# A two-layer message-passing kernel on one core: tiles processed 14 quads behind their visits, and the normalisation of message rows moved from VectorE to ScalarE

## The chip, the cores and the metric

The kernel runs on 1 core of one Trainium2 chip. The metric is the device time of that core in microseconds (us), as the median of the runs of one kernel. Times inside the kernel come from one profiled execution. The engines are named as in the profile: PE (TensorE matmul), PEld (its weight load), DVE (VectorE), ACT (ScalarE), POOL (GpSimd), SP (the engine that issues most DMAs); SPq, POOLq are their queues.

## The reference

A graph has 6,250 nodes with rows of 256 floats and 106,250 edges, sorted by destination, each with one weight. The first layer computes, for each edge, a message from the rows of both ends and the weight, sums messages by `src`, and updates the nodes:

```python
msg = silu(concat(h[src], h[dst], d2) @ mW1 + mb1)
msg = layer_norm(msg, ln_g, ln_b)
msg = silu(msg @ mW2 + mb2)
agg = segment_sum(msg, src, num_segments=6250)
y = silu(concat(h, agg) @ uW1 + ub1) @ uW2 + ub2
x = layernorm(x + (h + y))
# second layer: mean over the edges of x[src], by dst
agg = segment_sum(x[src], dst) / max(counts, 1)
x = layernorm(x + relu(agg @ W.T + b))
```

## The kernel before, in words

**Tiles, visits, quads.** The edges are cut into 831 tiles of 128, one edge to a partition; four tiles make a quad, and there are 208 quads of tiles (`TILE_QUADS`). The nodes are cut into 50 blocks of 125 (`BLOCKS`). A tile of sorted edges meets one or more blocks; each meeting is a "visit", of which there are 880, in 220 quads (`QUADS`). Tile t is complete once visit t + 49 is done (`BEHIND`).

**Preparation (0 to 222 us).** SP loads edges and weights, writes zeros into four sum tables in DRAM, and loads x. DVE and PE work out visits, blocks and ring slots (`vslot`, `vslot0`). Then `pq_step` runs over the 50 blocks: PE transposes x and multiplies it by both halves of mW1; the src half P goes to the table `p_tab` in DRAM, the dst half Q stays in SBUF as three bf16 parts in `big`. Last, SP issues `s_wrow`, a DMA that copies three partitions of the split weight row to three partitions of `big`, 50 times over (L407). POOL starts its gathers after `s_wrow`, after all stores of P, and after `s_q3`.

**First stage (222 to 2982 us), `step_0` and `message_loop`.** Each engine runs the same software pipeline in its own program order.

- POOL (`gather_0`, `add`): for each quad of tiles four indirect DMAs (L531) fetch P rows by src into a ring `ring0` of 60 slots; four indirect DMAs (L542) later add the finished rows `tot` into the four sum tables, by row numbers `sidx`. Gather g waits for the adds-in of quad g-4 (`pre`) and, once the ring is full, for the silu of the quad that held its slots.
- SP (`place_rows`): for each quad of visits it loads a row of local node numbers, copied to 125 partitions (`lrow`, L415), and three weight rows (L417).
- DVE: `one_hot` (L1234) makes the one-hot matrix; `add_in` (L1250) adds PE's result of a visit to its ring slot, four adds to a quad; `norm` takes `bn_stats` (L1259) of four silu'd rows, an inverse root by three Newton steps, and four `tensor_scalar` (L1282) that subtract the mean and scale; `count_before` (L1292) and `sum_rows` find duplicate source nodes and make `sidx`.
- PE: `norm_columns` (L701, transposes of the normalised rows), `sum_same` (L691), `expand` (L715: 12 matmuls that expand Q rows to the visit's edges), `keys` (L681), `main` (L727, L728: the product with mW2).
- ACT: two `silu` halves (L900), between them two evictions of transposes (L921), `total` (L936), `compare` (L910, L913), `message` (L928, the second silu).

At step q DVE adds in visit quad q + LAG and then normalises tile quad q; LAG is 13, so a tile quad is processed right after the add-in that completes it: `silu` of quad q waits for the `add_in` that DVE does at the same step. `expand` waits for all four adds of the visit quad before it, and signals once for all four.

**The rest (2982 to 4574 us).** The node update, the second layer's gathers and sums over the same visits (L570, L817, L1446), its projection, and the stores. The weight W of the second layer is loaded and transposed at the start (`wl`, `wt`, L597, L864).

Of the kernel before, what the change touches and what calls it, by code (L numbers as in the profile page):

```python
# [15 lines left out]
D = 256  # L16
# [29 lines left out]
RING0 = 60  # L46
RING0_QUADS = RING0 // QT
LAG = -(-BEHIND // QT)
assert RING - BEHIND < 4 * QT and RING0_QUADS == LAG + 2
# [3 lines left out]
def gnn(nc, x, src, dst, edge_w, mW1, mb1, ln_g, ln_b, mW2, mb2, uW1, ub1, uW2, ub2, W, b, out):  # L53
# [13 lines left out]
    with ExitStack() as ctx:  # L67
# [14 lines left out]
        wt = sb("wt", [P, H, D])  # L82
        b2r = sb("b2r", [P, D], bf16)
        blb = sb("blb", [P, D])
# [4 lines left out]
        RING0_W = RING0 * D  # L89
# [3 lines left out]
        ring0 = arena[:, BIG_W:BIG_W + RING0_W].rearrange("p (s d) -> p s d", s=RING0)  # L93
# [10 lines left out]
        vblk, vslot, vslot0, tslot = (vtab[32 * i:32 * i + 1, :] for i in range(4))  # L104
# [54 lines left out]
        wl = cut([H, D])  # L159
# [23 lines left out]
        region(LATE, 2048)  # L183
# [3 lines left out]
        ub2b = cut([D])  # L187

# [8 lines left out]
        nwt = sb("nwt", [P, 2, 4, QT])  # L197

# [33 lines left out]
        def by_place(rows_, group):  # L232
# [29 lines left out]
                 "keys", "silu", "bst", "mom", "newt", "norm", "ztr", "zev", "mm", "msg", "ded", "tot", "added"],  # L262
# [85 lines left out]
        def _(sp):  # L348
# [10 lines left out]
            for dest, arr in ((w1, mW1[0:2 * D, :]), (w2, mW2), (wl, W)):  # L359
                sp.dma_start(dest[:, :, :], arr.rearrange("(k p) d -> p k d", p=P)).then_inc(s_weights, 16)  # L360
            for dest, row in ((w1cf[:, 0, :], mW1[2 * D:2 * D + 1, :]), (b1b[:, :], mb1), (b2f[:, 0, :], mb2),
                              (blb[:, :], b)):
# [16 lines left out]
            def pq_step(q, k):  # L379
# [13 lines left out]
                if isinstance(q, int) and q == 0:  # L393
                    store_places()

            def store_places():
# [10 lines left out]
            sp.dma_start(big[NB:P, :, :, :].rearrange("p j k d -> p j (k d)"),  # L407
                         w1cp[0:PARTS, :, :].rearrange("p k d -> p (k d)").unsqueeze(1)
                         .to_broadcast([PARTS, BLOCKS, PARTS * D])).then_inc(s_wrow, 16)
            sp.wait_ge(s_vtab, 16 * 2 * (1 + PARTS))  # L410

            def place_rows(v, par):
                if later(v, 2):
                    sp.wait_ge(e[0]["qexp"], v - 1)
# [176 lines left out]
        def _(pe):  # L591
# [115 lines left out]
            def expand(q, par, blocks_):  # L707
# [3 lines left out]
                if later(q, 1):  # L711
                    pe.wait_ge(s["pre"], QT * q)
# [784 lines left out]
```

## Time and profile before

| | |
|---|---|
| median of 3 runs | 4588.72 us (4584.3 to 4591.06) |
| profiled execution, its own time | 4576.25 us |
| its span, first to last instruction | 4574.4 us |
| PE busy | 3282.8 us, 72% |
| POOL busy | 3025.7 us, 66% |
| DVE busy | 2739.4 us, 60% |
| ACT busy | 1443.1 us, 32% |
| mean granted TensorE clock | 0.858 of full speed |

Busy time is averaged over stages that have different limits; a stage has to be read by itself. The idle time in brackets ahead of an instruction names what ended it; "issue" means that the engine waited for nothing that the profile shows.

### The profile page before, as it was taken

How to read it: one execution, taken by the hardware profiler on the slowest of the kernel's cores; microseconds unless marked ns; L12 is line 12 of the kernel's file. 1: busy time of each engine (PE TensorE's matmuls, PEld its weight loads, DVE VectorE, ACT ScalarE, POOL GpSimd, SP SyncE). 2: the span in 40 equal slices, each digit the busy share in tenths (PEclk: the TensorE clock that was granted, in tenths of full speed). 3: DMA queues.
4: the chain of work that ended last, by engine and by line, in shares of the span. 5: the costliest groups of instructions: out<-in, count | busy, mean ns of one | idle time of the engine just before them, and what ended most of it. 6: DMA issues, size and time to landing. Idle time of an engine off the chain costs nothing. (4 is left out here: it accounts for less than half of the span.)

```text
span 4574.4 us, 77539 instructions
## 1 busy us (share of the span) xinstructions
PE 3282.8 (72%) x16047; PEld 2382.8 (52%) x16048; DVE 2739.4 (60%) x11915; ACT 1443.1 (32%) x2712; POOL 3025.7 (66%) x2631
## 2 busy tenths in 40 slices
PE   5737777777777777777777778686666666666675
PEld 2326666665656666666666666575333333343344
DVE  5437766666666666666666667567444444444455
ACT  0304444444444444444444445432000000000004
POOL 0057888888888888888888886521666666666634
PEclk8959888898989998888889889998777787777788
DMA  8335555555555555555555555754333333333313
GB/s 285 101 87 90 92 92 94 92 92 93 92 92 92 93 92 92 93 93 92 93 93 92 92 93 76 116 156 141 91 90 90 89 90 89 89 90 89 90 53 114
DMA packets 335844, 453.23 MB, mean 99 GB/s; under 512 B 53568, under 2 KB 282524, under 8 KB 335772
## 3 DMA queue, kind: packets, MB, share of 16 engines
q0 software_dynamic: 199680, 327.32, 38.4%
q1 hardware_dynamic: 136092, 125.14, 9.2%
q8 instruction: 22, 0.36, 0.0%
q14 instruction: 50, 0.41, 0.0%
HBM read 296.41 MB, written 155.62 MB: 99 GB/s over the span
## 5 line engine op out<-in xcount | busy, mean ns | idle before, releaser
L542 POOL DMA_INDIRECT sum<-arena,sidx x832 | 1327.9, 1596 | 320.3 <-issue 252.5
L531 POOL DMA_INDIRECT arena<-p_tab,esrc x832 | 819.9, 985 | 507.9 <-issue 249.9
L570 POOL DMA_INDIRECT arena<-x_tab,esrc x832 | 795.5, 956 | 473.7 <-issue 195.2
L817 PE MATMUL ps<-arena 128*125 x1760 | 696.9, 485 | 474.1 <-DVE arena L1446 249.6
L691 PE MATMUL ps<-arena 128*128 128x256 f32 x1664 | 560.4, 496 | 454.2 <-ACT arena L928 454.2
L727 PE MATMUL ps<-w,arena 128*128 128x256 f32 x3328 | 833.9, 383 | 17.5 <-ACT arena L936 17.4
L817 PEld LDWEIGHTS ps<-arena 128*125 128x125 f32 x1760 | 386.0, 237 | 771.0 <-issue 707.5
L1446 DVE TENSOR_TENSOR arena<-ps,arena 125x257 f32 x880 | 374.8, 426 | 617.1 <-remote 234.6
L691 PEld LDWEIGHTS ps<-arena 128*128 128x128 f32 x1664 | 389.2, 245 | 560.7 <-issue 495.7
L727 PEld LDWEIGHTS ps<-w,arena 128*128 128x128 f32 x3328 | 567.3, 190 | 136.9 <-issue 20.1
L910 ACT ACTIVATE arena<-ps,key 128x128 f32<-128x128 f32 x832 | 237.9, 369 | 1118.0 <-remote 1114.4
L1259 DVE BATCH_NORM_STATS2 bst<-arena 128x6 f32<-128x256 f32 x832 | 313.0, 418 | 389.5 <-ACT arena L900 384.9
L1250 DVE TENSOR_TENSOR arena<-ps,arena 128x256 f32 x880 | 372.9, 424 | 233.5 <-DVE arena L1250 84.4
L715 PE MATMUL ps<-arena 128*128 x2640 | 419.6, 322 | 83.0 <-DVE arena L1250 64.5
L991 ACT ACTIVATE arena<-ps 128x250 f32<-128x250 f32 x50 | 18.7, 375 | 1309.0 <-DVE cnt L1462 1309.0
L715 PEld LDWEIGHTS ps<-arena 128*128 128x128 bf16 x2640 | 309.0, 117 | 208.6 <-issue 117.0
L820 PE MATMUL ps<-identh 128*128 128x512 bf16 x880 | 399.3, 454 | 0.0
L1282 DVE TENSOR_SCALAR arena<-arena,mom,nwt 128x256 f32<-128x256 f32 x832 | 317.8, 442 | 99.9 <-DVE nwt L332 89.8
L701 PE MATMUL ps<-ident,arena 128*128 128x128 f32 x1664 | 228.4, 281 | 133.3 <-DVE arena L1282 108.9
L921 ACT ACTIVATE arena<-ps,gb 128x512 f32<-128x512 f32 x416 | 319.8, 769 | 7.8 <-PE ps L701 7.7
L701 PEld LDWEIGHTS ps<-ident,arena 128*128 128x128 f32 x1664 | 187.8, 143 | 186.0 <-DVE arena L1282 116.7
L900 ACT ACTIVATE arena<-arena 128x512 f32 x416 | 258.2, 621 | 35.1 <-DVE arena L1250 27.7
(177 smaller groups left out, 3927.8 us busy)
## 6 DMA issues: line engine op xcount, KB each, us to landing
arena<-loc_tab SPq DMA_DIRECT2D x220, 125.0 KB
sum<-arena SPq DMA_DIRECT2D x4, 6400.0 KB
arena<-sum SPq DMA_DIRECT2D x200, 128.0 KB, 2.1
arena<-p_tab,esrc POOLq DMA_INDIRECT x832
sum<-arena,sidx POOLq DMA_INDIRECT x832
arena<-x_tab,esrc POOLq DMA_INDIRECT x832
arena<-x_tab SPq DMA_DIRECT2D x50, 128.0 KB, 2.0
arena<-in_x_dram SPq DMA_DIRECT2D x50, 112.0 KB
```

The source lines that it names most:

```text
L531: pool.indirect_dma_start(out=ring0[:, tile % RING0, :], out_offset=None, in_=p_tab[:, :], in_offset=bass.IndirectOffsetOnAxis(ap=esrc[:, ...
L542: pool.indirect_dma_start(out=sums[u][:, :], in_=tot[:, par, u, :], in_offset=None, out_offset=bass.IndirectOffsetOnAxis(ap=sidx[:, par, u ...
L570: pool.indirect_dma_start(out=ring[:, tile % RING, 0:D], out_offset=None, in_=x1_tab[:, :], in_offset=bass.IndirectOffsetOnAxis(ap=esrc[:, ...
L691: last = nc.tensor.matmul(ps[:, PM + u // 2, u % 2 * D:(u % 2 + 1) * D], same[:, par, u, :], msg[:, par, u, 0:D], start=True, stop=True)
L701: last = nc.tensor.transpose(ps[:, PZ + h, u * P:(u + 1) * P], act[:, par, u, h * P:(h + 1) * P], ident[:, :])
L715: last = nc.tensor.matmul(ps[:, PP + u // 2, u % 2 * D:(u % 2 + 1) * D], hott[:, par, u, :], big[:, bass.ds(blocks_[u], 1), i, :].rearrang ...
L727: nc.tensor.matmul(to, zt[:, par, h, u * P:(u + 1) * P], w2[:, h, :], start=h == 0, stop=False)
L817: nc.tensor.matmul(ps[0:NB, u, 0:CW], same1[:, par, u, :], ring[:, bass.ds(at[u], 1), :].rearrange("p a c -> p (a c)"), start=True, stop=T ...
L820: nc.tensor.matmul(ps[:, PK, :], identh[:, :], identh[:, :].unsqueeze(1).to_broadcast([P, QT, P]), start=True, stop=True)
L921: nc.scalar.activation(zt[:, par, h, :], ps[:, PZ + h, :], ACT.Identity, bias=gb[:, h, 1:2], scale=gb[:, h, 0:1]).then_inc(s["zev"], 1)
L1250: nc.vector.tensor_tensor(row, ps[:, PP + u // 2, u % 2 * D:(u % 2 + 1) * D], row, ALU.add)\
L1446: nc.vector.tensor_tensor(row, ps[0:NB, u, 0:CW], row, ALU.add).then_inc(s["acc"], 1)
```

## The change

The lag between visits and tiles grows from 13 to 14 quads (`LAG`), and the ring from 60 to 64 slots, so that both layers share one table of slots. `silu` of a quad now waits for the add-in of DVE's previous step. `expand` waits and signals by pairs of visits (one PSUM bank each), and `add_in` takes them by pairs. DVE no longer applies the normalisation: it computes one small `shift` = -mean times scale, and ACT applies scale and shift with four activations, placed after `compare` and ahead of `message`. W, its transposes, its eviction and its bias move from the start to behind the first stage. The copy of the weight row (`s_wrow`) is issued in `store_places`, at block 0 of `pq_step`, rather than after block 49; the first two `place_rows` are issued at block 46.

```diff
-RING0 = 60
-RING0_QUADS = RING0 // QT
-LAG = -(-BEHIND // QT)
+LAG = -(-BEHIND // QT) + 1
@@ sync
-            for dest, arr in ((w1, mW1[0:2 * D, :]), (w2, mW2), (wl, W)):
+            for dest, arr in ((w1, mW1[0:2 * D, :]), (w2, mW2)):
...
+                if isinstance(q, int) and q == BLOCKS - 4:
+                    sp.wait_ge(s_vtab, 16 * 2 * (1 + PARTS))
+                    for v in range(2):
+                        place_rows(v, v)
@@ store_places
+                sp.wait_ge(s_wpart, 5)
+                sp.dma_start(big[NB:P, :, :, :].rearrange("p j k d -> p j (k d)"),
+                             w1cp[0:PARTS, :, :].rearrange("p k d -> p (k d)").unsqueeze(1)
+                             .to_broadcast([PARTS, BLOCKS, PARTS * D])).then_inc(s_wrow, 16)
@@ after the last block of pq_step
-            sp.wait_ge(s_wpart, 5)
-            sp.dma_start(big[NB:P, :, :, :].rearrange("p j k d -> p j (k d)"),
...
...
-            for dest, arr in ((u1, uW1), (u2, uW2)):
+            for dest, arr in ((u1, uW1), (u2, uW2), (wl, W)):
@@ gather_0
-                if g >= RING0_QUADS:
-                    pool.wait_ge(e[0]["silu"], 2 * (g - RING0_QUADS + 1))
+                if g >= RING_QUADS:
+                    pool.wait_ge(e[0]["silu"], 2 * (g - RING_QUADS + 1))
@@ expand (PE)
-                if later(q, 1):
-                    pe.wait_ge(s["pre"], QT * q)
                 for u in range(QT):
+                    if u % 2 == 0 and later(q, 1):
+                        pe.wait_ge(s["pre"], QT * q - 2 + u)
...
-                last.then_inc(s["qexp"], 1)
+                    if u % 2:
+                        last.then_inc(s["qexp"], 1)
@@ after the message loop (PE)
+            pe.wait_ge(s_late, 16 * 6)
+            pe.wait_ge(s["same"], TILE_QUADS)
+            for kd in range(H):
+                for kh in range(H):
+                    last = nc.tensor.transpose(ps[:, PK, (kd * H + kh) * P:(kd * H + kh + 1) * P],
+                                               wl[:, kh, kd * P:(kd + 1) * P], ident[:, :])
+            last.then_inc(s_wtr, 1)
+            pe.wait_ge(s_wt, 1)
@@ silu (ACT)
-                    ac.wait_ge(s["pre"], QT * (q + LAG + 1) if not isinstance(q, int) else QT * min(q + LAG + 1, QUADS))
+                    ac.wait_ge(s["pre"], QT * (q + LAG) if not isinstance(q, int) else QT * min(q + LAG, QUADS))
@@ ACT
+            def norm(q, par):
+                ac.wait_ge(s["shift"], q + 1)
+                for u in range(QT):
+                    last = nc.scalar.activation(act[:, par, u, :], act[:, par, u, :], ACT.Identity,
+                                                bias=shift[:, par, u:u + 1], scale=nwt[:, par, 3, u:u + 1])
+                last.then_inc(s["norm"], 1)
...
                 if live(q, TILE_QUADS):
                     compare(q, par)
+                if live(q, TILE_QUADS):
+                    norm(q, par)
                 if live(q - 1, TILE_QUADS):
                     message(q - 1, 1 - par)
@@ add_in (DVE)
-                dve.wait_ge(s["qexp"], v + 1)
                 for u in range(QT):
+                    if u % 2 == 0:
+                        dve.wait_ge(s["qexp"], 2 * v + 1 + u // 2)
@@ norm (DVE)
-                for u in range(QT):
-                    last = nc.vector.tensor_scalar(act[:, par, u, :], act[:, par, u, :], m[:, 4, u:u + 1],
-                                                   nwt[:, par, 3, u:u + 1], ALU.subtract, ALU.mult)
-                last.then_inc(s["norm"], 1)
+                nc.vector.scalar_tensor_tensor(out=shift[:, par, :], in0=m[:, 4], scalar=-1.0, in1=nwt[:, par, 3],
+                                               op0=ALU.mult, op1=ALU.mult).then_inc(s["shift"], 1)
```

## Rows read from the trace of the kernel before

**Rows 1.** The page: busy us, share of the span, and instructions of each engine.

```profile
PE 3282.8 (72%) x16047; PEld 2382.8 (52%) x16048; DVE 2739.4 (60%) x11915; ACT 1443.1 (32%) x2712; POOL 3025.7 (66%) x2631
```

**Rows 2.** Windows: us; busy of PE, PEld, DVE, ACT, POOL; PEclk, DMA share, GB/s.

```profile
222.50:351.90 129.40, 53.23 (x273) 35.26 (x274) 48.55 (x169) 13.15 (x24) 64.76 (x68) 0.59 0.31 86
351.90:2803.20 2451.30, 1889.77 (x10761) 1500.65 (x10762) 1686.50 (x8655) 1181.90 (x2117) 1981.16 (x1532) 0.90 0.56 92
2803.20:2982.00 178.80, 127.87 (x761) 102.57 (x758) 113.26 (x599) 86.31 (x150) 101.90 (x65) 0.93 0.62 96
```

**Rows 3.** Groups of POOL, 351.9 to 2803.2 us: busy, mean ns, idle before, releaser.

```profile
L542 POOL DMA_INDIRECT sum<-arena,sidx x768 | 1226.0, 1596 | 240.4 <-issue 233.9 <-ACT arena L936 6.6
L531 POOL DMA_INDIRECT arena<-p_tab,esrc x764 | 755.1, 988 | 232.8 <-issue 232.8
```

**Rows 4.** Timeline around 1400 us: start, us, instruction, idle before it.

```profile
1400.29 1.53 DVE L1282 TENSOR_SCALAR arena<-arena,mom,nwt 128x256 f32<-128x256 f32 x4 [0.87 <-DVE nwt L332]
1401.58 1.69 POOL L542 DMA_INDIRECT sum<-arena,sidx  x1 [0.30 <-issue]
...
1414.45 1.58 POOL L542 DMA_INDIRECT sum<-arena,sidx  x1 [0.30 <-issue]
```

**Rows 5.** Timeline: one `total` on ACT in the steady part.

```profile
1447.62 1.02 ACT L936 ACTIVATE arena<-ps 128x1024 f32<-128x1024 f32 x1 [0.79 <-DMA sum<-arena,sidx]
```

**Rows 6.** Timeline: from the last block of `pq_step` to the first gather.

```profile
209.81 0.93 SPq L407 DMA_DIRECT2D arena<-arena  x1
210.05 0.42 ACT L882 ACTIVATE arena<-arena 125x256 bf16<-125x256 f32 x1 [0.27 <-DVE arena L1207]
210.50 0.42 DVE L1213 TENSOR_TENSOR arena<-arena 125x256 bf16<-125x256 f32 x1 [0.24 <-ACT arena L882]
...
217.85 2.00 SPq L417 DMA_DIRECT2D arena<-wgt_tab  x1
222.51 1.18 POOL L531 DMA_INDIRECT arena<-p_tab,esrc  x1 [216.55 <-DMA arena<-arena]
```

**Rows 7.** DMA queue of SP, 211 to 222.2 us: packets, MB, share of 16 engines.

```profile
q1 hardware_dynamic: 364, 0.44, 18.3%
```

**Rows 8.** Timeline: the first blocks of `pq_step`.

```profile
96.08 0.58 SPq L403 DMA_DIRECT2D wgt_tab<-arena  x1
98.20 0.78 SPq L391 DMA_DIRECT2D p_tab<-arena  x2
101.61 0.42 DVE L1204 TENSOR_TENSOR arena<-ps,arena 125x256 f32<-125x256 f32 x1 [0.21 <-PE ps L667]
```

**Rows 9.** Waits of POOL, 222 to 352 us: us in total, times, longest.

```profile
POOL arena L531 <- ACT arena L900: 23.6, 2, 18.3
POOL arena L531 <- DVE arena L1250: 17.9, 9, 6.7
```

**Rows 10.** Timeline: first adds of visit quads 2, 12, 13; `expand` of quad 13.

```profile
256.77 0.42 DVE L1250 TENSOR_TENSOR arena<-ps,arena 128x256 f32 x1 [16.59 <-remote]
...
320.17 0.42 DVE L1250 TENSOR_TENSOR arena<-ps,arena 128x256 f32 x1 [1.90 <-PE ps L715]
...
322.58 2.74 PE L715 MATMUL ps<-arena 128*128 x12 [2.62 <-DVE arena L1250]
...
325.53 0.42 DVE L1250 TENSOR_TENSOR arena<-ps,arena 128x256 f32 x1 [2.18 <-PE ps L715]
```

**Rows 11.** Timeline after the last gather: POOL's first scatter of three quads; ACT, PE.

```profile
2835.47 1.68 POOL L542 DMA_INDIRECT sum<-arena,sidx  x1 [3.20 <-DVE sidx L1311]
2835.89 1.03 ACT L928 ACTIVATE arena<-ps 128x1024 f32<-128x1024 f32 x1 [2.53 <-PE ps L728]
2842.20 1.10 PE L727 MATMUL ps<-w,arena 128*128 128x256 f32 x4 [1.21 <-ACT arena L936]
2909.19 1.68 POOL L542 DMA_INDIRECT sum<-arena,sidx  x1 [2.99 <-DVE sidx L1311]
2974.77 1.55 POOL L542 DMA_INDIRECT sum<-arena,sidx  x1 [3.05 <-DMA sum<-arena,sidx]
```

More of the change, by code:

```diff
@@ L103, in gnn @@
         vtab = sb("vtab", [P, VISITS], i32)
-        vblk, vslot, vslot0, tslot = (vtab[32 * i:32 * i + 1, :] for i in range(4))
+        vblk, vslot, tslot = (vtab[32 * i:32 * i + 1, :] for i in range(3))
         esrc = sb("esrc", [P, CHUNKS * P], i32)
@@ L187, in gnn @@
         ub2b = cut([D])
+        wl = cut([H, D])
+        wt = cut([H, D])
+        blb = cut([D])
         scr = sb("scr", [P, QT, P])
@@ L197, in gnn @@
         nwt = sb("nwt", [P, 2, 4, QT])
+        shift = sb("shift", [P, 2, QT])
         tnum_i = sb("tnum_i", [P, CHUNKS], i32)
@@ L261, in gnn @@
         EDGE = [["gat0", "gat1", "gat2", "gat3", "loc0", "loc1", "wgt0", "wgt1", "hott", "keyt", "apart", "same", "dup", "dif", "sidx", "qexp", "pre",
-                 "keys", "silu", "bst", "mom", "newt", "norm", "ztr", "zev", "mm", "msg", "ded", "tot", "added"],
+                 "keys", "silu", "bst", "mom", "newt", "shift", "norm", "ztr", "zev", "mm", "msg", "ded", "tot", "added"],
                 ["hot", "agg", "acc"]]
@@ L394, in pq_step, with place_rows @@
                     store_places()
+                if isinstance(q, int) and q == BLOCKS - 4:
+                    sp.wait_ge(s_vtab, 16 * 2 * (1 + PARTS))
+                    for v in range(2):
+                        place_rows(v, v)
+            def place_rows(v, par):
+                if later(v, 2):
+                    sp.wait_ge(e[0]["qexp"], 2 * (v - 1))
+                sp.dma_start(lrow[0:NB, par, :], loc_tab[:, bass.ds(v * (QT * P), QT * P)].to_broadcast([NB, QT * P]))\
+                    .then_inc(e[0][f"loc{par}"], 16)
+                sp.dma_start(hott[NB:P, par, :, :].rearrange("p u n -> p (u n)"),
+                             wgt_tab[:, bass.ds(v * (QT * P), QT * P)]).then_inc(e[0][f"wgt{par}"], 16)
             def store_places():
@@ L592, in _ @@
             pe.wait_ge(s_const, 10)
-            pe.wait_ge(s_weights, 16 * 11)
-            for kd in range(H):
-                for kh in range(H):
-                    last = nc.tensor.transpose(ps[:, PK, (kd * H + kh) * P:(kd * H + kh + 1) * P],
-                                               wl[:, kh, kd * P:(kd + 1) * P], ident[:, :])
-            last.then_inc(s_wtr, 1)
-            pe.wait_ge(s_wt, 1)
+            pe.wait_ge(s_weights, 16 * 9)
             def tile_before(tile, prev):
@@ L862, in _ @@
         def _(ac):
-            ac.wait_ge(s_wtr, 1)
-            nc.scalar.activation(flat(wt[:, :, :]), ps[:, PK, :], ACT.Copy).then_inc(s_wt, 1)
             def pq_step(q, par):
@@ L952, in step_0 @@
                     compare(q, par)
+                if live(q, TILE_QUADS):
+                    norm(q, par)
                 if live(q - 1, TILE_QUADS):
                     message(q - 1, 1 - par)
-            ac.wait_ge(s_weights, 16 * 11)
+            ac.wait_ge(s_weights, 16 * 9)
             ac.wait_ge(s_constc, 8)
             message_loop(ac, step_0)
+            ac.wait_ge(s_wtr, 1)
+            nc.scalar.activation(flat(wt[:, :, :]), ps[:, PK, :], ACT.Copy).then_inc(s_wt, 1)
             t = k[0]
```

71 lines of the change are left out of this document (28 added, 43 removed).

## The prediction

> **What bounds the kernel now.** I read the page first: over the whole span PE is the busiest engine, at 72%, and POOL comes behind it at 66% [rows 1]. That average hides the answer, so I cut the span into windows by stage [rows 2] and then asked for POOL's groups in the long middle of the first stage [rows 3]. The two groups are 1226.0 + 755.1 us of work and 240.4 + 232.8 us of gaps, together 2454 us in a window of 2451.3: POOL does nothing but issue indirect DMAs. All but 6.6 us of its gaps are "issue", 466.7 us over 1532 instructions, 0.30 us each. It never waits there for a gather slot, for `tot` or for `sidx`. From the first scatter (351.9) to that of quad 192 (2803.2) are 192 iterations of 2451.3 / 192 = 12.77 us: 4 scatters of 1.596, 4 gathers of 0.988 and 8 gaps. The rest follows POOL: ACT's `total` is let go by the landing of a scatter [rows 5], which means that the chain of DVE, ACT and PE is ahead by as much as its buffers allow.
>
> Two short parts are not bound so. At the head, from the first gather to the first scatter (129.4 us, [rows 2]), POOL does 17 quads of gathers at 64.76 / 68 = 0.95 us and a gap of 0.30 each, so 5.0 us a quad and 85 in all; 44 us are idle, and [rows 9] name who is late: `silu` of quads 0 and 1 (23.6) and the adds-in (17.9), each with the usual gap in it; the rest is the first `total`. After the last gather the scatters wait 3 us a quad [rows 11]: from quad 195 (2835.47) to quad 202 (2909.19) are seven periods of 10.53 us. There the chain is the bound. The second layer is not touched.
>
> So the question for each part of the change is when POOL starts, what its iterations cost, and how long the chain takes at either end.
>
> **1. The start of the gathers.** Before, `pq_step` ends at 210.92 on DVE, but POOL starts at 222.51, let go by the copy L407, issued at 209.81 [rows 6]. From issue to release are 12.7 us. While it runs, SP's queue uses 18.3% of 16 DMA engines [rows 7], close to 3/16 = 18.8%: three engines, one per partition copied. The loads that SP issues behind it are held up as well (L417 takes 2.00 us to issue, [rows 6]). The Trainium skill ("DMA: Bandwidth & Descriptors", section on why a DMA increments its semaphore by 16) says that the number of engines is the largest up to 16 that divides the slowest dimensions, and that each engine takes its descriptors in ring order; the share in the trace agrees.
>
> After, the same copy is issued in `store_places`, behind the last `wgt_tab` store (96.08 to 96.66, [rows 8]), ahead of the load of block 4 and the store of block 0, both of which also use these three engines. So it is paid there: issued at 96.7, it ends, by its 12.7 us, at 109.4. The store of block 0, issued at 98.20 now, frees the buffer that DVE needs for block 2 at 101.61 [rows 8]. That add moves to about 109.8: 8.2 us later. Nothing in `pq_step` catches up, since 48 blocks from there to 210.50 take 2.27 us each [rows 6, 8]. Removing the load of W and its bias (384 KB) from the queue ahead of four zeroed tables of 6.6 MB each, which is 1.5% of what must pass in the 85 us or so before the x rows, gives 1.2 back. The gathers then wait for the last store of P, about 1 us after DVE: 210.9 + 8.2 - 1.2 + 1 = 218.9 instead of 222.5. **-3.5 us.** Bounds: -11.5 if the copy is hidden in `pq_step`, 0 if it delays by all 12. PE's four transposes and ACT's eviction at the start lie beside the zero fill, and the slot arithmetic that DVE drops too: 0. At their new place they lie beside POOL's last scatters: 0; uncovered, 2 us.
>
> **2. The head.** Visits go in lockstep now: four adds, then 12 matmuls that wait 2.62 us for them and take 2.74 [rows 10], at a granted clock of 0.59 [rows 2], near the lower level of 1.2 GHz: 5.36 us a quad (320.17 to 325.53). By pairs the two overlap: 1.0 us of adds, 1.4 of matmuls and 0.6 of signals for a pair, 3.0 us for a quad. POOL's 5.01 becomes the pace. The stalls stay: quad 2 is added in only at 256.77 after 16.59 us of "remote" [rows 10], and others of 2 to 5 us every third quad; why, no row tells. Adds of quad 13 end some 2.2 us after their start at 325.53, at 327.7, 105 us after the first gather. With the stalls kept and catching up at 3.0, I get 81.5 us if only the first counts (34 + 8 quads x 5.01 + landing and adds) and 101 if each stall comes at its old time. I take 90, nearer the middle. From there to the first scatter are 24.2 us, two passes of the chain, which term 4 shortens by about a tenth: 22. Head: 112 instead of 129.4, **-17.4**, bounds -4 and -28. One more gather quad lies inside it, in POOL's idle time.
>
> **3. POOL's iteration.** DVE's four L1282 disappear. [Rows 4] show that a scatter which starts while they run takes 1.69 us, and one in the next iteration, which starts as they start, 1.58: 0.11 for a hit. One hit in two iterations to one in each gives 0.055 to 0.11; I take 0.077, so 12.69 us. 190 iterations: **-14.6**; bounds 0 (the hit moves to another DVE instruction) and -30. Here the Trainium skill speaks up ("SBUF — State Buffer", section "SBUF: two separate sides"): a DVE instruction in a two-port mode keeps GpSimd off the shared port for the whole instruction, so it can't write descriptors. By that rule 1.53 us of L1282 in each iteration could be up to 290 us in the stage; the row says 0.11 per hit.
>
> ACT's share grows: a 256-wide activation takes 0.42 us alone [rows 6]; four in a row 1.2 to 1.7, I take 1.4. ACT is busy 1181.9 / 192 = 6.2 us of 12.77 [rows 2]; 7.6 after. `message` of the quad before is queued behind it, and `sum_same` on PE waits for that. Covered: POOL's pace leaves the chain at least 12.77 - 10.53 = 2.2 us an iteration. The lag itself buys nothing here, since nobody waits for the chain.
>
> **4. The tail.** Its loop now: DVE's adds, `silu`, statistics, Newton, L1282 (1.4 to 1.5 us for four, [rows 4]), and on ACT and PE `message`, `sum_same`, `total`, then `main`, which waits 1.21 us for `total` [rows 11]. After, `silu` no longer waits for adds (about 1.7 us), and DVE sheds 1.3. From one `main` to the next: message 1.03, two silus and two evictions 2.9, total 1.0 with its signals, and 4.14 of matmuls make 9.25; but statistics 0.75, Newton to `shift` 4.2 and ACT's 1.4 behind the second silu end at 9.55. I take 9.55 (bounds 9.2 and 10.3). Before, from the scatter of quad 190 to that of 207 (2974.77) are 2 x 12.77 + 171.6 = 197.1 us, with 14.8 beyond the regular period while x rows are loaded. After, one quad more is without gathers: 10 + 16 x 9.55 + 14.8 = 177.6. **-19.5**, bounds -8 and -24.
>
> **Sum.** -3.5 - 17.4 - 14.6 - 19.5 = -55. Against the profiled execution: its own time 4576.25 becomes 4521, span 4519. The median of the runs is 12.5 us above that execution; I take the same difference for the change: 4588.7 - 55 = **4534**.
>
> **Rivals.**
> A. Only the ends give a little: POOL's iteration stays at 12.77 and the stalls of the head come at their old times: -3.5 - 4 - 0 - 12 = -20, **4569**. For it: the stalls had no cause in view, and other DVE instructions can hit. 0.20.
> B. POOL was slowed by DVE in more than the visible hits. Its floor by the means of the windows with least beside them is 4 x 1.57 (101.90 / 65 in the tail) + 4 x 0.95 (64.76 / 68 in the head) + 8 x 0.30 = 12.48 [rows 2], so -55 in place of -14.6: **4493**. 0.08. This is how far the skill's rule on the shared port could come in; full exclusion would have to show in [rows 4], and doesn't.
> C. Slower: DVE, free of its waits, settles where L1292, L1234 and the small operations fall on POOL's starts. Each hit costs 0.11 or more; the ends give 40 us, so it decides from 0.21 us an iteration, two hits more than now. At three new hits of 0.12 and the old one lost, +0.28 an iteration is +54 us, less the 40 of the ends: 14 slower than before, **4603**. Against it: those instructions exist today at all phases, and the mean is only 0.29 above that floor. 0.04.
> D. Nothing measurable: the early copy holds `pq_step` by more than 12 us, the head's stalls grow by what the pairs save, and the tail stays bound by `main`: -8, **4581**. 0.10.
> That the lag does nothing by itself in the steady part is in every case.
>
> **Numbers.** Forecast 0.58, A 0.20, B 0.08, C 0.04, D 0.10. About 0.2% (9 us) is what a measurement of this kernel can tell. Faster: forecast, A, B, which is 0.86, less 0.01 for A's edge: 0.85; same 0.11; slower 0.04. The forecast's own range, from the bounds in part: 4507 to 4560. To leave out no more than 2 in 10 it must hold A: 4500 to 4574.
>
> **What would show it.** The page after: POOL's first gather near 219; the copy's engines busy near 98 to 110 and DVE waiting there for a store of P; DVE's visits at 5.0 us or less a quad in the head; first scatter near 331; POOL's steady groups still with "issue" gaps only, means 1.57 to 1.59 and 0.98; tail periods near 9.6 us; ACT near 1730 us busy, DVE near 2400. Wrong would make it: POOL waiting for `tot` or `sidx` in the steady part, a period off 12.69 by more than 0.1, or a head as long as now.

## The result, and the profile after

The changed kernel takes 4685.88 us (median of 4 runs, 4681.7 to 4699.55). The kernel before takes 4589.89 beside it (4 runs, 4584.3 to 4591.94). That is a ratio of 1.0222, 95% interval 1.0209 to 1.0234. It is 2.2% slower. The forecast was 4534 and faster.

The page of the profiled execution has a span of 4685.7 us and these busy times, to be held against [rows 1]:

```profile
PE 3327.0 (71%) x16047; PEld 2460.8 (53%) x16048; DVE 2462.8 (53%) x11287; ACT 1859.4 (40%) x3544; POOL 3008.0 (64%) x2631
```

Work moved from DVE to ACT as foretold, and POOL is even 18 us less busy. So nothing became longer on POOL; it waited more. The windows by stage say where: first gather to first scatter, then to the last gather, then to the copy of the x rows (us; busy of PE, PEld, DVE, ACT, POOL; PEclk, DMA share, GB/s).

```profile
220.55:346.93 126.38, 57.41 (x282) 36.48 (x283) 47.30 (x166) 17.04 (x31) 68.50 (x73) 0.59 0.34 93
346.93:2886.17 2539.24, 1878.83 (x10643) 1537.50 (x10641) 1416.97 (x7993) 1548.76 (x2850) 1946.51 (x1519) 0.86 0.54 88
2886.17:3091.42 205.25, 153.40 (x879) 123.88 (x876) 111.59 (x636) 132.34 (x241) 113.19 (x73) 0.90 0.60 93
```

The middle holds 190 iterations: 2539.24 / 190 = 13.36 us each, where [rows 2] give 12.77. POOL's groups in it (busy, mean ns, idle before, releaser), beside [rows 3]:

```profile
L544 POOL DMA_INDIRECT sum<-arena,sidx x760 | 1202.5, 1582 | 366.9 <-issue 223.4 <-ACT arena L945 143.5
L533 POOL DMA_INDIRECT arena<-p_tab,esrc x759 | 744.0, 980 | 231.3 <-issue 231.0 <-DMA sum<-arena,sidx 0.3
```

Each scatter got shorter, 1582 ns for 1596 (why is another matter, see step 3 below), and 143.5 us of waits for ACT's `total` (L945) appeared where there were 6.6. POOL no longer sets the pace in every iteration; in 37 of about 120 between 1000 and 2600 us it waits for the chain of ACT, PE and DVE. The list of waits, 1000 to 2600 us (total us, times, longest), shows its links:

```profile
ACT arena L912 <- remote: 440.2, 77, 7.1
PE ps L697 <- ACT arena L921: 409.7, 87, 6.7
...
POOL sum L544 <- ACT arena L945: 86.6, 37, 3.4
```

L912 is `compare`, L921 the normalisation, L697 PE's transposes of the normalised rows. "Remote" means that the trace shows no instruction ending just before the wait ended. The timeline of two steps tells what that wait is:

```profile
1418.87 1.14 ACT L912 ACTIVATE arena<-ps,key 128x128 f32<-128x128 f32 x4 [6.43 <-remote]
1420.05 0.72 ACT L915 ACTIVATE arena<-arena,onesf 128x512 f32<-128x512 f32 x1
1420.68 2.06 ACT L921 ACTIVATE arena<-arena,shift,nwt 128x256 f32<-128x256 f32 x4
1422.64 1.00 ACT L937 ACTIVATE arena<-ps 128x1024 f32<-128x1024 f32 x1
1422.79 1.97 PE L697 MATMUL ps<-ident,arena 128*128 128x128 f32 x8 [5.80 <-ACT arena L921]
...
1424.55 2.90 PE L687 MATMUL ps<-arena 128*128 128x256 f32 x8
1427.29 1.47 PE L711 MATMUL ps<-arena 128*128 x12
1428.60 0.61 PE L677 MATMUL ps<-identh,keyh 128*128 128x128 bf16 x8
...
1432.45 1.14 ACT L912 ACTIVATE arena<-ps,key 128x128 f32<-128x128 f32 x4 [3.85 <-remote]
```

PE's keys matmuls (L677) end at 1429.21, and `compare`, which waits for them, begins at 1432.45, 3.24 us later; the one before began 5.84 us late (its matmuls are at 1412.42, 0.61 long). Behind `compare` in ACT's queue stands the normalisation, 2.06 us, and PE waits for that: a ring, keys, `compare`, normalisation, L697, `sum_same`, `expand`, keys. From `compare` at 1418.87 to keys at 1428.60 is 9.73 us, so one turn is that, 0.61 of keys, and the lateness. The lateness is not the same in every step: between 1000 and 2600 us it is under 1.3 us in 36 of 120.

From all rows of `compare` and of the keys matmuls in that window, the mean turn comes apart into two parts. In the kernel before, 7.85 us from the start of `compare` to the end of the next keys, and 4.94 of lateness, make 12.78, which is POOL's own iteration. In the changed kernel it is 9.91 and 3.45, which make 13.36. So the ring took in 2.06 us, the length of the normalisation, and the lateness gave 1.49 of them back.

By stage, up to the last scatter (before, then after): first gather 222.51, 220.55; head 129.4, 126.4; last scatter 2980.36, 3089.82. So 109 of the 111 us that the span grew lie ahead of the last scatter: 114 between the first scatter and the last, less the 5 gained ahead of the first. That the ring turns too slowly because the normalisation stands behind a late `compare` is called Theory A below. Theory B is that the 14 quads behind or the two signals a quad cost it.

### The profile page after: what moved, and what is told of

Same layout as the page of the kernel before. It is cut to its first block and busy times, and to the rows that moved or that the text cites. A ratio compares the mean times of both kernels' runs of the same rounds, so it can differ in the third digit from the quotient of the medians.

```text
span 4685.7 us, 78432 instructions
## 1 busy us (share of the span) xinstructions
PE 3327.0 (71%) x16047; PEld 2460.8 (53%) x16048; DVE 2462.8 (53%) x11287; ACT 1859.4 (40%) x3544; POOL 3008.0 (64%) x2631
## 5 line engine op out<-in xcount | busy, mean ns | idle before, releaser
L821 PE MATMUL ps<-arena 128*125 x1760 | 716.8, 497 | 447.4 <-DVE arena L1457 214.8
L697 PE MATMUL ps<-ident,arena 128*128 128x128 f32 x1664 | 330.1, 363 | 690.4 <-ACT arena L921 682.3
L821 PEld LDWEIGHTS ps<-arena 128*125 128x125 f32 x1760 | 403.1, 245 | 749.0 <-issue 680.9
L697 PEld LDWEIGHTS ps<-ident,arena 128*128 128x128 f32 x1664 | 261.0, 187 | 770.4 <-ACT arena L921 581.9
L912 ACT ACTIVATE arena<-ps,key 128x128 f32<-128x128 f32 x832 | 237.7, 368 | 789.1 <-remote 689.3
L687 PEld LDWEIGHTS ps<-arena 128*128 128x128 f32 x1664 | 417.9, 264 | 100.2 <-issue 24.4
L921 ACT ACTIVATE arena<-arena,shift,nwt 128x256 f32<-128x256 f32 x832 | 428.3, 585 | 30.6 <-DVE shift L1294 29.6
L824 PE MATMUL ps<-identh 128*128 128x512 bf16 x880 | 412.9, 469 | 0.0
L711 PE MATMUL ps<-arena 128*128 x2640 | 351.1, 286 | 68.4 <-DVE arena L1263 45.2
L711 PEld LDWEIGHTS ps<-arena 128*128 128x128 bf16 x2640 | 269.4, 102 | 147.0 <-issue 82.7
L945 ACT ACTIVATE arena<-ps 128x1024 f32<-128x1024 f32 x208 | 212.9, 1024 | 213.3 <-PE ps L687 128.9
```

Source lines behind the costliest of these rows:

```text
L687: last = nc.tensor.matmul(ps[:, PM + u // 2, u % 2 * D:(u % 2 + 1) * D], same[:, par, u, :], msg[:, par, u, 0:D], start=True, stop=True)
L697: last = nc.tensor.transpose(ps[:, PZ + h, u * P:(u + 1) * P], act[:, par, u, h * P:(h + 1) * P], ident[:, :])
L711: last = nc.tensor.matmul(ps[:, PP + u // 2, u % 2 * D:(u % 2 + 1) * D], hott[:, par, u, :], big[:, bass.ds(blocks_[u], 1), i, :].rearrang ...
L821: nc.tensor.matmul(ps[0:NB, u, 0:CW], same1[:, par, u, :], ring[:, bass.ds(at[u], 1), :].rearrange("p a c -> p (a c)"), start=True, stop=T ...
L824: nc.tensor.matmul(ps[:, PK, :], identh[:, :], identh[:, :].unsqueeze(1).to_broadcast([P, QT, P]), start=True, stop=True)
L921: last = nc.scalar.activation(act[:, par, u, :], act[:, par, u, :], ACT.Identity, bias=shift[:, par, u:u + 1], scale=nwt[:, par, 3, u:u + 1])
```

## The experiments

The runs came on different chips, and that turned out to be part of the finding. I call the chip of the result A; B to F are five chips of the later runs, all different. Which chip A is was not noted. B, C, D and F give the kernel before other times than A does, but E gives nearly the same and may be the same chip. Each ratio is against the kernel before on the same chip. "POOL" is its iteration: the window 1000 to 2600 us has so many POOL instructions, 8 to an iteration, so 12800 over their number. "Late" is from the end of the keys matmuls to `compare`, 1000 to 1400 us, mean; it is left out where it was not taken, or (norm first) where ACT's own order makes it. In e6 ACT's own order makes the 1.1 too. The runs of e9 to e12 are two each.

| run | chip | us | before there | ratio (95%) | POOL | late |
|---|---|---|---|---|---|---|
| kernel before | A | 4589.89 | | 1 | 12.76 | 5.0 |
| changed kernel | A | 4685.88 | 4589.89 | 1.0222 (1.0209 to 1.0234) | 13.38 | 3.5 |
| e1 norm on DVE | B | 4360.52 | 4373.23 | 0.9968 (0.9955 to 0.998) | 12.70 | 0.1 |
| e2 before, ACT norm | B | 4367.43 | 4373.23 | 0.9986 (0.9977 to 0.9996) | 12.71 | |
| e3 norm first | B | 4351.51 | 4373.23 | 0.9949 (0.9932 to 0.9965) | 12.64 | |
| e4 one signal | B | 4355.25 | 4373.23 | 0.9954 (0.9937 to 0.997) | 12.65 | |
| e5 changed kernel | C | 4352.32 | 4373.67 | 0.9949 (0.9932 to 0.9966) | 12.65 | 0.1 |
| e6 kernel before | C | 4372.89 | 4373.67 | one run | 12.76 | 1.1 |
| e7 changed, 2 loads | C | 4382.08 | 4373.67 | 1.0019 (1.0009 to 1.003) | 12.66 | 2.9 |
| e8 before, 2 loads | C | 4362.81 | 4373.67 | 0.9973 (0.9963 to 0.9983) | 12.71 | 3.1 |
| e9 changed, 4 loads | D | 5464.07 | 4555.83 | 1.1994 (1.1959 to 1.2029) | 17.02 | 6.1 |
| e10 norm first, 4 loads | D | 4907.1 | 4555.83 | 1.0771 (1.0688 to 1.0855) | 14.24 | 5.4 |
| e11 DVE norm, 4 loads | D | 4972.25 | 4555.83 | 1.0914 (1.0832 to 1.0996) | 14.68 | 6.3 |
| e12 before, 4 loads | D | 5020.21 | 4555.83 | 1.102 (1.0976 to 1.1063) | 14.78 | 6.1 |
| e13 changed kernel | E | 4697.18 | 4583.2 | 1.0257 (1.0239 to 1.0274) | 13.36 | 3.6 |
| e14 kernel before | E | 4586.41 | 4583.2 | one run | 12.77 | 4.9 |
| e15 norm first | E | 4583.8 | 4583.2 | 1.0004 (0.9995 to 1.0014) | 12.83 | |
| e16 norm on DVE | E | 4578.64 | 4583.2 | 0.9988 (0.9978 to 0.9998) | 12.79 | 4.9 |
| e17 keys last | F | 4755.99 | 4372.28 | 1.0877 (1.0859 to 1.0895) | 14.50 | 0.1 |
| e18 one signal | F | 4351.75 | 4372.28 | 0.9954 (0.9937 to 0.997) | 12.64 | 0.1 |

**e1, e2, e3, e4: the parts.** The edits, each by itself (e2 on the kernel before, the others on the changed one):

```diff
@@ e1: L1294 back to DVE's four instructions, and no norm on ACT
-                nc.vector.scalar_tensor_tensor(out=shift[:, par, :], in0=m[:, 4], scalar=-1.0, in1=nwt[:, par, 3],
-                                               op0=ALU.mult, op1=ALU.mult).then_inc(s["shift"], 1)
+                for u in range(QT):
+                    last = nc.vector.tensor_scalar(act[:, par, u, :], act[:, par, u, :], m[:, 4, u:u + 1],
+                                                   nwt[:, par, 3, u:u + 1], ALU.subtract, ALU.mult)
+                last.then_inc(s["norm"], 1)
@@ e2: the reverse of e1, in the kernel before, norm(q, par) behind compare(q, par)
@@ e3: step_0 of ACT
                 if live(q, TILE_QUADS):
-                    compare(q, par)
-                if live(q, TILE_QUADS):
                     norm(q, par)
+                if live(q, TILE_QUADS):
+                    compare(q, par)
@@ e4: expand and add_in, one wait and one signal a quad
-                    if u % 2 == 0 and later(q, 1):
-                        pe.wait_ge(s["pre"], QT * q - 2 + u)
+                    if u == 0 and later(q, 1):
+                        pe.wait_ge(s["pre"], QT * q)
...
-                    if u % 2:
-                        last.then_inc(s["qexp"], 1)
+                    if u == QT - 1:
+                        last.then_inc(s["qexp"], 2)
...
-                    if u % 2 == 0:
-                        dve.wait_ge(s["qexp"], 2 * v + 1 + u // 2)
+                    if u == 0:
+                        dve.wait_ge(s["qexp"], 2 * v + 2)
```

> The changed kernel, with the normalisation given back to VectorE (four tensor_scalar a quad, no shift, no norm on ScalarE); lag 14, 64 slots, pairs and the moved DMAs stay. Theory A (ScalarE's normalisation is queued behind compare, which starts late, and makes the chain of DVE, ACT and PE longer than POOL's iteration): POOL has only its 0.30 us gaps again, an iteration is about 12.75 us against 13.37, and the time is 4575 to 4592. Theory B (the new lag and the signals by pairs disturb the chain): it stays at about 4680.

> The kernel before, with only the normalisation moved to ScalarE, in the place that the change gives it (after compare, ahead of message); lag 13, 60 slots. Theory A: as slow as the changed kernel or slower, 4680 to 4800, since silu still waits for the adds-in of its own step. Theory B: about 4590, the same as before.

> The changed kernel, with ScalarE's norm placed ahead of compare instead of behind it; nothing else. Theory A: the late start of compare no longer holds up the normalisation, so much of the loss comes back: iteration 12.8 to 13.1, time 4590 to 4640. If it is only ScalarE's 2.06 us of work and not the place, or theory B: 4670 to 4700.

> The changed kernel, with expand waiting and signalling once for all four visits again, and the adds-in waiting once. Theory A: within 10 us of the changed kernel's 4686, perhaps a little slower at the head. Theory B: back towards 4590.

Measured: all four took 0.1 to 0.5% less than the kernel before, and in all four POOL's gaps are its usual 0.3 us. On chip B the kernel before takes 4373 us, not 4590. So Theory A missed for e2 and e4, where it wanted a slow kernel, and Theory B missed for e1 and e3, where it wanted one. Neither could be judged before the changed kernel itself had run on such a chip.

**e5, e6: both kernels again, e7, e8: a made lateness.** e7 and e8 add, to the changed kernel and to the kernel before, two loads one behind the other:

```diff
@@ SP, step_0, behind place_rows
+                if live(q, TILE_QUADS):
+                    sp.wait_ge(e[0]["keyt"], q + 1)
+                    sp.dma_start(late[:, 0, :], x[0:1, 0:4]).then_inc(e[0]["rel0"], 16)
+                    sp.wait_ge(e[0]["rel0"], 16 * (q + 1))
+                    sp.dma_start(late[:, 1, :], x[0:1, 0:4]).then_inc(e[0]["rel1"], 16)
@@ ACT, compare
                 ac.wait_ge(s["keyt"], q + 1)
+                ac.wait_ge(s["rel1"], 16 * (q + 1))
```

> The changed kernel itself, unchanged, on the chip that runs these four. The changed kernel lost 2.2% against the kernel before on the first chip, while four versions near it gained 0.1 to 0.6% on the second one. Theory A (ACT's normalisation is queued behind a compare that begins late, because PE's keys signal is seen 5 to 6 us late while gathers run): what the change does depends on whether that lateness is there; where compare begins within 0.5 us of the end of the keys matmuls, the changed kernel takes 0.4 to 0.6% less than the kernel before (4350 to 4356 us beside 4373), and where it begins 5 to 6 us behind, 2.2% more. Theory B (14 quads behind the visits, or the two signals of expand, cost the 115 us by themselves, on any chip): 2% slower here too, with POOL waiting in each iteration.

> The kernel before, unchanged, for its trace on this chip. Theory A: it takes the same time as the runs of it beside; where this chip's compares begin within 0.5 us of the keys matmuls in the changed kernel, they do so here too. POOL's iteration is 12.7 to 12.8 us either way, since nothing on the chain of the visits is queued behind compare in this kernel.

> The changed kernel, with the keys signal made late: SP waits for it, loads four numbers from DRAM, waits for them, loads four more, and ACT's compare waits for the second load; some 4 to 5 us of lateness in every quad, and two small transfers. Theory A: ACT's normalisation, queued behind compare, moves back with it, PE's transposes of the normalised rows and the message behind them too, and the iteration of the first stage grows from 12.7 us to 13.2 or more: at least 90 us more than the changed kernel without it. Theory B: lateness of compare costs nothing; within 15 us of the changed kernel.

> The kernel before with the same two loads between the keys signal and compare. Theory A: nothing of the normalisation stands behind compare on ACT but the message, and DVE's count of equal keys; compare has some 6 us of room, so it takes the time of the kernel before within 15 us, and POOL's iteration stays 12.7 to 12.8 us. Theory B says the same. If both this one and the changed kernel with the loads grow, the loads themselves or SP's wait are what costs, and the pair tells nothing of the order on ACT.

The changed kernel, not a line different, is 0.5% faster on chip C: Theory B, as a cost on any chip, falls. The timeline of e5 has the difference (compare with the one above):

```profile
1418.10 1.14 ACT L912 ACTIVATE arena<-ps,key 128x128 f32<-128x128 f32 x4 [0.73 <-PE ps L677]
1419.28 0.72 ACT L915 ACTIVATE arena<-arena,onesf 128x512 f32<-128x512 f32 x1
1422.94 2.07 ACT L921 ACTIVATE arena<-arena,shift,nwt 128x256 f32<-128x256 f32 x4 [2.94 <-DVE shift L1294]
```

`compare` is let go by L677 itself, and ends before DVE's `shift` is there; the normalisation waits 2.94 us for that (1.22 in the next step). That is the room a late `compare` has. e7 agrees: 2.9 us of lateness left POOL at 12.66, so its expectation of 90 us or more missed. Its 30 us over e5 lie outside the steady part but for 3 (head 105.1 for 101.8, last gather to last scatter 222.2 for 204.0, the rest later). e8 came out 11 us under the kernel before, all of it ahead of the last scatter; why, I did not follow.

**e9 to e12: the lateness of chip A.** The same with four loads, on the changed kernel, on e3, on e1 and on the kernel before.

> The changed kernel with a chain of four small loads, in place of two, between the keys signal and compare: two loads gave 2.5 to 3.4 us of lateness and 30 us in all, so four should give 5 to 6.5 us, the lateness of the first chip. Theory A (the normalisation waits on ACT behind the late compare): the first stage's iteration goes to 13.2 us or more, the kernel to 4445 us or more, if this chip is as the second one (kernel before at 4373). Theory B (what the first chip lost came from something else that its late signals only accompany): within 40 us of the changed kernel.

> The changed kernel with ACT's normalisation ahead of compare, and the same chain of four loads. Theory A: the late compare now holds back only itself, the message and the count of equal keys; less time than the changed kernel with the four loads, by 40 us or more. If the two take the same time within 15 us, the lateness costs through the message or the count of equal keys, and not through the normalisation's place in ACT's queue.

> The changed kernel with the normalisation back on DVE, and the four loads. Theory A: as with the normalisation ahead of compare, nothing of the chain silu, normalise, transpose is queued behind compare; 40 us or more below the changed kernel with the four loads. Rival: 14 quads behind or the two signals of expand are what cannot stand the lateness; the same as the changed kernel with the four loads within 15 us.

> The kernel before with the four loads. Theory A: within 15 us of the kernel before without them, as it took 6 us of lateness in each quad on the first chip with POOL never short of work for it. If it grows as much as the changed kernel, the loads cost by themselves.

With lateness above 5 us in every step the changed kernel falls to 17.02 us an iteration. Its waits, 1000 to 2600 us, are the same links as on chip A:

```profile
ACT arena L920 <- DMA late<-in_x_dram: 637.6, 94, 8.1
PE ps L704 <- ACT arena L929: 534.8, 89, 7.3
POOL sum L551 <- ACT arena L953: 437.9, 94, 5.7
```

Norm first takes 2.78 us less an iteration, norm on DVE 2.34 less, both as Theory A had it. But e12 missed: the kernel before went to 14.78, not 12.8. It has a ring of its own, keys, `compare`, `message`, `sum_same`, `expand`, keys. The room for 6 us that I saw in it was not there: on chip A every step was late already and the turn was 7.85 + 4.94 us, with nothing to spare; in e12 it is 8.63 + 6.16. Between e9 and e12 are 17.02 - 14.78 = 2.24 us, close to the 2.06 of ACT's normalisation: that is what the change puts into the ring. The made lateness is not the natural one in all, though. It is above 5 us in every step, where that of chip A gave way when the ring grew. And neither kernel was traced on chip D without the loads, so e9 to e12 compare with one another only.

**e13 to e16: no loads, on a chip with late compares.**

> The changed kernel itself, for its trace and time on the chip of these four. Theory A: on a chip where compare begins 3 to 6 us behind the keys matmuls (there the kernel before takes 4550 to 4590 us) it is 1.5 to 2.5% slower than the kernel before; on one where compare begins at once (the kernel before at 4373) it is 0.4 to 0.6% faster.

> The kernel before, for its trace on this chip: with compare 3 to 6 us behind the keys matmuls where the kernel takes 4550 to 4590 us, and 1 us behind where it takes 4373. POOL's iteration 12.7 to 12.8 us on either.

> The changed kernel with the normalisation ahead of compare in ACT's queue. Theory A: on a chip with late compares the lateness holds nothing of the chain silu, normalise, transpose back; within 0.5% of the kernel before (0.9 to 1.1 us of each late step come back as longer DVE waits at most), and 1.5% or more under the changed kernel. Rival: if it is within 0.3% of the changed kernel there, the place of the normalisation on ACT is not the cause, and the loss comes from the 14 quads behind or the pair of signals.

> The changed kernel with the normalisation on DVE: the schedule of 14 quads behind and the pair of signals alone. Theory A: on a chip with late compares within 0.5% of the kernel before, on the others 0.3% under it. Rival (the lag or the two signals cost the 2%): as slow as the changed kernel on a chip with late compares.

This is the deciding set. The changed kernel loses 2.6% on chip E. With two calls swapped on ACT (e15) it takes the time of the kernel before, 113 us less. With the norm on DVE and all else changed (e16), it takes 119 less. So neither the 14 quads behind nor the two signals cost anything there, and the normalisation costs it only behind `compare`. The waits of the changed kernel (e13), 1000 to 2600 us:

```profile
ACT arena L912 <- remote: 424.7, 75, 7.2
PE ps L697 <- ACT arena L921: 410.7, 87, 6.7
...
POOL sum L544 <- ACT arena L945: 89.4, 39, 3.6
```

the same of the kernel before (e14), where the wait is the longest of all and yet POOL, whose gaps are all "issue", never waits for the chain:

```profile
ACT arena L910 <- remote: 728.8, 124, 7.4
...
PE ps L691 <- ACT arena L928: 290.8, 122, 4.1
POOL sum L542 <- issue: 153.7, 500, 0.9
```

and of e15, where the normalisation waits for DVE alone:

```profile
ACT arena L921 <- DVE shift L1294: 394.2, 110, 5.4
...
POOL sum L544 <- issue: 156.4, 492, 1.0
```

**e17, e18.** e17 puts PE's `keys` behind `main`; e18 is e4 again.

```diff
@@ PE, step_0
-                if live(q, TILE_QUADS):
-                    keys(q, par)
                 if live(q - 1, TILE_QUADS):
                     main(q - 1, 1 - par)
+                if live(q, TILE_QUADS):
+                    keys(q, par)
```

> The changed kernel with PE's keys matmuls behind main instead of ahead of it, so that PE has nothing to issue behind them but a wait. On two chips compare began 5 to 6 us behind the keys matmuls, about when main behind them had ended. Theory H1 (a signal is seen late as long as PE goes on with matmuls behind it): compare begins within 0.5 us of the end of keys, which is where it began before, and the kernel takes within 30 us of the changed kernel on such a chip. Theory H2 (the signal is late by a fixed 5 to 6 us whatever follows): compare begins 5 us later still, and the kernel takes 100 us or more over the changed kernel. On a chip without late compares (kernel before at 4373) it says only what 5 us of later keys cost: POOL would be short of work in part, 20 us or more over the changed kernel's 4352.

> The changed kernel with one wait and one signal in the expansion of a quad, in place of two. On a chip with late compares: Theory A, the second signal has no part in the 2.2%, 4670 to 4700 us as the changed kernel. Rival: the extra signal is what PE's signals are late by; then it comes down by 50 us or more, and the gap from keys to compare shrinks. On a chip without them: 4355 us as in the first run.

Chip F has no late compares, so H1 and H2 were not told apart, and the second signal was not taken out alone on a chip that has them (e16 keeps it there and is not slow). But e17 shows the ring without any odd signal: `compare` is prompt and only its matmuls are later, by the length of `main`, some 4 us.

```profile
1420.76 0.61 PE L677 MATMUL ps<-identh,keyh 128*128 128x128 bf16 x8
1421.49 1.14 ACT L912 ACTIVATE arena<-ps,key 128x128 f32<-128x128 f32 x4 [4.85 <-PE ps L677]
1423.29 2.06 ACT L921 ACTIVATE arena<-arena,shift,nwt 128x256 f32<-128x256 f32 x4
1425.40 1.97 PE L697 MATMUL ps<-ident,arena 128*128 128x128 f32 x8 [4.03 <-ACT arena L921]
...
1435.10 0.61 PE L677 MATMUL ps<-identh,keyh 128*128 128x128 bf16 x8
```

The turn shown is 14.34 us, POOL follows at 14.50, and the kernel is 404 us over the changed kernel on chip C.

## Why the prediction was wrong, by its own steps

**Step 3, the cover of ACT's share, failed, and it alone turned the sign.** The text had: "POOL's pace leaves the chain at least 12.77 - 10.53 = 2.2 us an iteration". The 10.53 was read in the tail, where `compare` begins within 1.2 us of its matmuls. In the steady part of the same trace (kernel before, chip A) it began 3.0 to 6.3 us behind in all 125 steps from 1000 to 2600 us, and the wait was in the list of waits:

```profile
ACT arena L910 <- remote: 741.9, 125, 6.9
```

I had named `message` and `sum_same` as what stands behind the new instructions on ACT, but not asked what stands ahead of them. Ahead stood the engine's longest wait. The chain had no 2.2 us to spare there, but nothing: its turn was 12.78 us already. Two sizes were off as well: the normalisation took 2.06 us where I had 1.4, and its cost was not 0 but 13.36 - 12.69 = 0.67 us in each of 190 iterations, 127 us. From the scatter of quad 0 to that of quad 190 the kernel grew by 112.2 us, where step 3 had -14.6. e15 and e16 show that the place of the normalisation, and no other part, made the kernel slower on chip E; for chip A it rests on the same waits and the same turn. The forecast did name POOL waiting for `tot` as the sign that would make it wrong, and that sign came.

**Step 3, the hits on POOL: a near number by another mechanism, which is luck.** POOL's iteration went from 12.76 to 12.65 on chip C, 0.11 for a forecast 0.08, and scatters took 1582 ns, within "1.57 to 1.59". But the forecast put the gain down to L1282 hitting the scatters, and e1 and e2 say otherwise. The scatters of e1, where the four L1282 are back, stay as short as those of the changed kernel. Those of e2, where they are gone from the kernel before, stay as long as there (1000 to 2600 us):

```profile
L544 POOL DMA_INDIRECT sum<-arena,sidx x504 | 797.6, 1582 | 153.6 <-issue 152.7 <-ACT arena L902 0.9
L543 POOL DMA_INDIRECT sum<-arena,sidx x504 | 804.5, 1596 | 153.6 <-issue 153.6
```

So the shorter scatters came with the rest of the change, by what isn't shown (not the two signals: e4 has 1581 ns). The four DVE instructions cost the iteration about 0.05 us, 12.70 in e1 against 12.65 in e4 on the same chip, and that in the gathers, 985 ns against 973. By the two-port rule of the Trainium skill ("SBUF — State Buffer", "SBUF: two separate sides") up to 290 us could have come back. 0.05 us in 190 iterations is 10 us; whether L1282 runs in a two-port mode at all, no run here shows.

**Step 1, the start: -3.5 forecast, -2.0 measured.** The early copy (L416) did hold DVE up. In the changed kernel:

```profile
95.58 0.94 SPq L416 DMA_DIRECT2D arena<-arena  x1
...
108.39 0.42 DVE L1216 TENSOR_TENSOR arena<-ps,arena 125x256 f32<-125x256 f32 x1 [6.63 <-DMA p_tab<-arena]
```

108.39 stands against 101.61 in [rows 8], 6.8 us later; I had 8.2.

**Step 2, the head: -17.4 forecast, -3.0 measured.** The stalls were taken as partly caught up. They stayed, in another form, and this term failed by 14 us:

```profile
248.53 0.42 DVE L1263 TENSOR_TENSOR arena<-ps,arena 128x256 f32 x1 [10.07 <-remote]
...
259.85 0.42 DVE L1263 TENSOR_TENSOR arena<-ps,arena 128x256 f32 x1 [7.67 <-remote]
```

On chip C the head takes 100.8 us before and 101.8 after, with no "remote" wait at all: the 29 us between the chips in the kernel before go with these stalls. There the pairs buy nothing, since 17 quads of gathers at 5.0 us are 85 of the 101 us. Had I read [rows 10] as the sign of late signals and looked for the same releaser elsewhere, I should have met `compare`.

**Step 4, the tail: -19.5 forecast, +2.2 measured.** From the scatter of quad 190 to that of quad 207 are 194.6 us before and 196.8 after. (The forecast had 197.1 before: it counted the period from quad 191 to 192 as 12.77, which was 10.37 already. Its 9.25 for the loop that it thought the shorter one is 9.07 by its own terms.) After the last gather the period became

```profile
2899.97 1.57 POOL L544 DMA_INDIRECT sum<-arena,sidx  x1 [5.30 <-ACT arena L945]
...
2910.10 1.56 POOL L544 DMA_INDIRECT sum<-arena,sidx  x1 [2.97 <-DMA sum<-arena,sidx]
...
2920.19 1.55 POOL L544 DMA_INDIRECT sum<-arena,sidx  x1 [2.95 <-DMA sum<-arena,sidx]
...
2931.61 1.55 POOL L544 DMA_INDIRECT sum<-arena,sidx  x1 [4.28 <-DVE sidx L1322]
```

10.1 and then 11.4 us. I had left out that a scatter waits for the landings of the quad before: 4 scatters of 1.56 and 3 gaps of 0.3 are 7.1 us, and 2.97 of landing make 10.1, above my 9.55. So these two periods came out only 0.4 us under the old one, and a later one waits for `sidx`.

**The rivals.** A was nearest for the ends, C had the right sign by a wrong mechanism (no new hits; scatters got shorter). None had a wait ahead of ACT's new work in its queue. On the chips without late compares the kernel is 0.5% faster, by 21 us of the 55 forecast.

## What to carry to other kernels

Before work is put into an engine's queue, look at what stands ahead of it as well as behind: an in-order engine's longest wait, harmless while nobody needs what follows it, becomes part of every ring that the new work is in. Measure the room of a chain in the stage where it will be used; here the same chain seemed to have 2.2 us to spare by the tail, and had none in the steady part of chip A. And where a placement costs nothing, put the work with the urgent consumer first: e15, two calls swapped, is the best choice here over both kinds of chip (0.5% faster than the kernel before on B, the same on E), with e16 beside it.

## What the runs showed of the hardware

**Signals of PE arrive late on some chips.** In one and the same kernel (before), `compare` begins 1.1 us behind its matmuls on chip C (all 31 steps from 1000 to 1400 us 1.06 to 1.14, which is ACT's own order) and 2.8 to 6.4 us on chip E. It isn't ACT: SP, which waits for the signal of `expand`, is late too. Kernel before, chip E:

```profile
1409.77 1.47 PE L715 MATMUL ps<-arena 128*128 x12
1411.08 0.61 PE L681 MATMUL ps<-identh,keyh 128*128 128x128 bf16 x8
1414.72 0.26 SPq L415 DMA_DIRECT2D arena<-loc_tab  x1
...
1417.68 1.14 ACT L910 ACTIVATE arena<-ps,key 128x128 f32<-128x128 f32 x4 [6.57 <-remote]
```

and chip C:

```profile
1413.02 1.72 PE L715 MATMUL ps<-arena 128*128 x12 [1.41 <-DVE arena L1250]
1414.68 0.61 PE L681 MATMUL ps<-identh,keyh 128*128 128x128 bf16 x8
1414.91 0.26 SPq L415 DMA_DIRECT2D arena<-loc_tab  x1
```

3.5 us behind the end of `expand` on E, 0.2 on C. On A the lateness of `compare` ends with the last gather. Nor is it PE alone: on A and E DVE waits up to 1.3 us for signals of its own (L1282 for L332, 81 times and 60.1 us on A from 1000 to 2600 us), on C never over 0.3.

**The late signals keep POOL's time.** In the kernel before on chip A, the end of the keys matmuls wanders by 3 us against POOL, and `compare` doesn't. In 124 of 125 steps from 1000 to 2600 us the nearest end of a POOL instruction is that of the second scatter, and `compare` begins 0.06 us behind it in the mean (on E 114 of 125). The second scatters of two steps stand in [rows 4] (1401.58 and 1.69 long, 1414.45 and 1.58 long); here are the rest:

```profile
1398.11 0.61 PE L681 MATMUL ps<-identh,keyh 128*128 128x128 bf16 x8
1403.37 1.14 ACT L910 ACTIVATE arena<-ps,key 128x128 f32<-128x128 f32 x4 [6.08 <-remote]
...
1409.43 0.61 PE L681 MATMUL ps<-identh,keyh 128*128 128x128 bf16 x8
1416.14 1.14 ACT L910 ACTIVATE arena<-ps,key 128x128 f32<-128x128 f32 x4 [6.67 <-remote]
```

In the changed kernel on A the same split shows: keys that end during the gathers (66 of 120 steps) are seen 4.1 to 6.7 us late, those that end in the first scatter (54) 1.0 us in the mean. In the kernel before all 63 waits above 0.6 us of DVE for its own inverse root end during a first or second scatter as well. That is why its `compare` is always late and costs nothing: it comes at a fixed point of POOL's iteration, however early the keys are. H1, that the signal is late as long as PE goes on with matmuls, fits less well. In 28 of the 125 steps `compare` begins before `main` has ended, and in the second step above PE had ended `main` at 1413.99, stood idle to 1416.00, and the signal was still out. Whether the scatters hold the signals up, or both follow something else, was not tested; moving POOL's scatters on chip A would be the test. The clock is no answer by itself, since e17 runs at 0.848 of full speed without late signals and e14 at 0.849 with them.

**Chips differ more than the change does, and by the same waits.** The kernel before takes 4372 to 4374 us on B, C and F, 4556 on D, 4583 on E and 4590 on A. Every trace of A, D and E has "remote" waits, and no trace of B, C and F has one. D has them too: none ahead of `compare` in e9 to e12 (SP issued its first load within 0.1 us of the keys' end), but 213 to 250 us of them on DVE in the second layer, where no loads were added. Of the 214 us between E and C (e14 and e6), 34 lie ahead of the last scatter, most of it the stalls of the head. 169 lie in the second layer's gathers, which take 1216.6 us on E and 1047.4 on C from the first to the last; there DVE has 208.6 us of "remote" waits on E.

**Four 256-wide activations with scale and bias from SBUF take 2.06 us in a row**, 0.52 each, where one alone, of another form (bf16 out), had taken 0.42 [rows 6].
